# Coefficients of an eight-step graph layer from powers of one symmetric matrix, with an earlier load and a redrawn order of stages

## The reference

```python
# x: (16, 512, 128), adj: (512, 512); four layers, each followed by a layernorm
x = layernorm(x + L0(x))   # ((x + relu(G(relu(G(x)))))/2, G(x) = x W_loop + adj (x W_neigh) + b
x = layernorm(x + L1(x))
x = layernorm(x + L2(x))   # concat of x scaled by row sums (adj, adaptive softmax) @ W + b
x = layernorm(x + L3(x))   # attention over 256 edges: leaky_relu, segment softmax, scatter

# L1, with N_STEPS = 8
h = jnp.einsum('bnd,ed->bne', x, fc_in_w) + fc_in_b
w_eff = w * d_clamped @ w.T
dt = jnp.float32(SPATIAL_SCALE / N_STEPS)
def euler_step(h, _):
    ax = jnp.einsum('nm,bmd->bnd', adj_mx, h)
    f = alph * 0.5 * (ax - h) + h @ w_eff - h + x0
    return (h + dt * f, None)
h, _ = jax.lax.scan(euler_step, h, None, length=N_STEPS)
```

## Time and profile before

| | |
|---|---|
| median of 3 runs | 724.84 us (724.22 to 725.11) |
| profiled execution | 727.18 us, span 725.3 us |
| granted TensorE clock, mean | 0.901 |
| PE busy | 597.7 us (82%) |
| DVE busy | 466.0 us (64%) |
| ACT busy | 331.2 us (46%) |
| POOL busy | 220.2 us (30%) |

### The profile page before, as it was taken

How to read it: one execution, slowest core, us unless ns; L and a number is a source line. 1 busy time by engine, 2 the same in 40 slices (tenths; PEclk the granted TensorE clock), 3 DMA queues, 4 the chain that set the end, 5 groups by cost and what they waited for, 6 DMA issues and landing times.

```text
span 725.3 us, 9315 instructions
## 1 busy us (share of the span) xinstructions
PE 597.7 (82%) x3024; PEld 504.5 (70%) x3024; DVE 466.0 (64%) x1256; ACT 331.2 (46%) x777; POOL 220.2 (30%) x222
## 2 busy tenths in 40 slices
PE   2768849689999999996885859899999999785662
PEld 2556618558997889974774747789887998674541
DVE  6883677235464576537798779726639662678665
ACT  2661211464725367424285354663544752264132
POOL 1252502252216311232155343450552122302402
PEclk9897758789999999997898999999999999987676
DMA  7100000300000000211031110400000011001122
GB/s 221 33 0 30 0 1 0 117 1 0 2 1 1 1 1 1 83 34 59 3 114 59 58 59 1 117 1 1 1 0 1 1 67 51 0 1 59 58 58 59
DMA packets 28502, 24.61 MB, mean 34 GB/s; under 512 B 3739, under 2 KB 22683, under 8 KB 28453
## 3 DMA queue, kind: packets, MB, share of 16 engines
q1 hardware_dynamic: 27012, 19.25, 8.7%
...
...
## 4 chain that ended last, share of the span: by engine, by line
PE 60%; DVE 28%; ACT 5%; issue 3%; POOL 2%; DMA 1%; ACTq 0%; DVEq 0%; POOLq 0%
PE bank L1260 32%; PE bank L1542 11%; DVE stats L1076 6%; PE bank L1459 5%; PE bank L1458 4%; ACT ZH L624 2%; PE bank L1434 2%; PE bank L1446 1%; PE bank L1515 1%; POOL ZL L540 1%; DVE XF L1167 1%; DVE XF L1241 1%; PE bank L1328 1%; POOL small L563 1%; DVE XF L1094 1%
## 5 line engine op out<-in xcount | busy, mean ns | idle before, releaser
L563 POOL TENSOR_TENSOR small<-small,minus_half 128x8 f32<-128x8 f32 x32 | 55.1, 1722 | 314.4 <-DVE small L1069 314.4
L540 POOL TENSOR_TENSOR ZL<-XF,ZH 128x512 fp32r<-128x512 f32 x64 | 80.9, 1299 | 105.8 <-ACT ZH L624 105.8
L624 ACT ACTIVATE ZH<-bank 128x128 fp32r<-128x128 f32 (+1 forms) x112 | 35.8, 323 | 110.4 <-PE bank L1260 109.9
L1048 DVE TENSOR_TENSOR ZL<-bank,ZH 128x128 fp32r<-128x128 f32 (+1 forms) x112 | 37.7, 345 | 69.7 <-ACT XF L624 53.4
L813 ACT ACTIVATE XF<-XF,small 128x128 f32<-128x128 f32 x128 | 52.0, 486 | 53.1 <-POOL small L565 46.8
L1260 PE MATMUL bank<-QH,YR 128*128 128x384 f32 x256 | 75.9, 337 | 0.0
L1459 PE MATMUL bank<-ZL,BTH 128*128 128x512 f32 x192 | 74.3, 418 | 0.0
L1458 PE MATMUL bank<-ZH,BTH 128*128 128x512 f32 x144 | 61.0, 423 | 2.1 <-POOL ZL L540 2.0
L1076 DVE BATCH_NORM_STATS2 stats<-XF 128x6 f32<-128x128 f32 x256 | 55.8, 281 | 2.2
L1542 PE MATMUL bank<-ZH,RH 128*128 128x512 f32 x128 | 51.1, 399 | 1.7 <-POOL ZL L540 0.8
L1542 PE MATMUL bank<-ZH,RL 128*128 128x512 f32 x128 | 50.7, 396 | 0.0
...
## 6 DMA issues: line engine op xcount, KB each, us to landing
...
Z<-x_rows,ends_at POOLq DMA_INDIRECT x16, 3.5
...
```

The costliest lines, as they stand in the source:

```text
L540: g.tensor_tensor(lo, whole, raw(hi), ALU.subtract).then_inc(pool_done[s], 1)
L563: g.tensor_tensor(sm[:, 6, :], sm[:, 5, :], minus_half[:, :], ALU.pow).then_inc(pool_done[s], 1)
L624: return A.activation(out_, in_, ACT.Copy, **more)
L1048: ins = (v.tensor_tensor(lo, part, raw(hi), ALU.subtract) if shift is None else v.scalar_tensor_tensor(lo, part, shift, raw(hi), ALU.add, ...
```

## The change

- Powers. V2, V3 and V4, V5 to V8 are made as plain powers of V in three small stages, `w.pw0`, `w.pw1` and `w.pw2`, which stand apart from each other in the order. ACT copies each power, scaled by a binomial, into VC (eight copies). POOL fills SV with multiples of the identity at the very start. DVE adds the powers into SV with 28 instructions on 128 by 128 elements (`w_sums`, in its stage `w.q`).
- Q. PE makes each of the three lots of Q as one product of FCN with three blocks of VC and one of CENTRE with three of SV (384 columns each; the last lot is two blocks wide, and one block more with the identity). The banks are those of stream 0.
- `row_sum` moves on DVE from the end of `w.weights` to the end of `w.lmat`.
- Scratch of the preparation moves out of the buffer of x of group 1. SP issues that load at once behind the first loads, and its transposed twin at `w.one_hot`.
- The order is redrawn. In the preparation, `0.pair2` and `0.neigh2` stand ahead of `w.r3`, and `1.x0`, `1.t0` and `1.neigh1` stand ahead of `w.end`. In the middle of turn 0, `0.gather`, `0.qv` and `0.score` stand ahead of `1.giant2`. At the end of turn 1, `2.l2.b` alternates with `3.lot.b`, `2.norm.2` stands behind `3.lot.3`, and `2.gather` stands behind `3.giant2`.
- Some waits are added where buffers or banks are shared in a new way, among them `step1` of group 0 on DVE's "done" and `neigh1` of group 1 on `weights`.

```diff
--- before.py
+++ after.py
@@ -154,8 +157,8 @@
         regions = {"F1": flat(F[1]), "ZH1": flat(ZH[1]), "ZL1": flat(ZL[1]), "TH1": flat3(TH[1]),
-                   "TL1": flat3(TL[1]), "X1": flat(X[1]), "Y1": Y[1][:, :],
-                   "T1": T1[:, :], "Q": Q[:, :]}
+                   "TL1": XT[1][:, :], "X1": flat(X[1]), "Y1": Y[1][:, :],
+                   "Q": Q[:, :]}
...
-        in_order = """w.adj w.low w.w0 w.v 0.x0 w.lmat 0.t0 0.neigh1 w.r2 0.conv1 w.edges w.r3 w.rt w.powers w.one_hot
...
+        in_order = """w.adj w.low w.w0 0.x0 w.v w.lmat w.pw0 0.t0 0.neigh1 w.r2 w.pw1 0.conv1 w.edges 0.triple 0.stats.0
...
@@ -474,9 +474,10 @@
             load_weights("w")
             load_weights("ends")
-            def w_end():
-                sync.wait_ge(w_dve_done, after(w_dve_steps, 0, "done"))
-                load(1, 1)
+            load(1, 1)
+
+            def w_one_hot():
+                sync.wait_ge(w_dve_done, after(w_dve_steps, 0, "one_hot"))
                 load_t(1, 1)
@@ -533,6 +534,8 @@
+            for k in range(EULER_STEPS):
+                link(g.tensor_scalar(SV[:, k, :], ident[:, :], DT + (1.0 if k == 0 else 0.0), None, ALU.mult))
@@ -600,20 +603,9 @@
-            def w_q():
-                gp.wait_ge(w_dve_done, after(w_dve_steps, 0, "r_lo", NB - 1))
-                for factor in factors:
-                    link(g.tensor_scalar(ident_by[factor], ident[:, :], factor, None, ALU.mult))
@@ -684,9 +676,28 @@
+            def by_choice(p, src):
+
+                k = EULER_STEPS - p
+                copy(VC[:, k, :], src, scale=float(comb(EULER_STEPS, k))).then_inc(w_act_done, 1)
+
+            def w_pw0():
+                ac.wait_ge(w_dve_done, after(w_dve_steps, 0, "v"))
+                by_choice(1, V)
+                ac.wait_ge(w_dve_done, after(w_dve_steps, 0, "v2"))
+                by_choice(2, power[:, 0, :])
...
@@ -910,6 +926,7 @@
+                v.tensor_reduce(row_sum, adj_sb, AX, ALU.add).then_inc(w_dve_done, 1)
@@ -976,16 +993,36 @@
-            def w_powers():
...
+            def w_pw0():
+                dv.wait_ge(w_dve_done, after(w_dve_steps, 0, "row_sum"))
+                dv.wait_ge(w_pe_done, after(w_pe_steps, 0, "v2"))
+                v.tensor_copy(power[:, 0, :], w_bank[3][:, 0:D]).then_inc(w_dve_done, 1)
...
+            def w_sums():
+
+                nonlocal n
+                dv.wait_ge(w_pool_done, after(w_pool_steps, 0, "const"))
+                dv.wait_ge(w_dve_done, after(w_dve_steps, 0, "v8"))
+                for p in range(1, EULER_STEPS):
+                    if p > 1:
+                        dv.wait_ge(dve_chain, n)
+                    v_p = V if p == 1 else power[:, p - 2, :]
+                    for k in range(EULER_STEPS - p):
+                        v.scalar_tensor_tensor(SV[:, k, :], v_p, DT * comb(k + p, k), SV[:, k, :],
+                                               ALU.mult, ALU.add).then_inc(dve_chain, 1)
+                        n += 1
...
@@ -1004,7 +1041,7 @@
-                v.tensor_reduce(row_sum, adj_sb, AX, ALU.add).then_inc(w_dve_done, 1)
+                v.memset(tmp_c, 0.0).then_inc(w_dve_done, 1)
...
@@ -1353,68 +1395,65 @@
+            def w_pw0():
+                pt.wait_ge(w_dve_done, after(w_dve_steps, 0, "nv1_t"))
+                products(w_bank[3][:, 0:D], [(V, V)]).then_inc(w_pe_done, 1)
...
             def w_q():
-                pt.wait_ge(w_pool_done, after(w_pool_steps, 0, "q"))
-                pt.wait_ge(w_dve_done, after(w_dve_steps, 0, "t_sum", NB - 1))
...
                 for i in range(LOTS):
-                    for place in range(LOT):
-                        k = place * LOT + i
...
-                        last = products(w_bank[i][:, block_of(place)],
-                                        [(f_power, scaled(f_factor))]
-                                        + [(power(j - k, 1), scaled(factor)) for j, factor in parts])
+                    n = LOT if i < LOTS - 1 else LOT - 1
+                    last = products(q_bank(i)[:, 0:n * D], [(FCN, VC[:, i::LOT, :]), (CENTRE, SV[:, i::LOT, :])])
+                    if n < LOT:
+                        last = products(q_bank(i)[:, n * D:LOT * D], [(FCN, ident[:, :])])
...
+                if (turn, s, stage, i) == (0, 0, "step1", 0):
+                    pt.wait_ge(w_dve_done, after(w_dve_steps, 0, "done"))
+                if (turn, s, stage, i) == (0, 1, "neigh1", 0):
+                    pt.wait_ge(w_dve_done, after(w_dve_steps, 0, "weights"))
```

More of the change, by code:

```diff
@@ new lines, in w_numbered @@
+        def w_numbered(steps):
+            return numbered([one for name in in_order if name[:2] == "w." for one in steps.get(name[2:], [])])
+        w_dve_done = sem("w_dve_done")
+        w_dve_steps = w_numbered({
+            "adj": [("b_hi", NB), ("r_diag", 1)], "low": [("b_lo", NB), ("r_row", 1)], "w0": [("inexact", 1)],
+            "v": [("w_by_d", 1), ("v", 1), ("centred", 1), ("nv1_t", 1)],
+            "lmat": [("l_nat", NB), ("l_lo", NB), ("row_sum", 1)], "r2": [("l2", NB), ("l2_lo", NB)],
+            "edges": [("perm", 1), ("ends_row", 1), ("src_col", 1)], "r3": [("l3", NB)], "rt": [("r_lo", NB)],
+            "pw0": [("v2", 1)], "pw1": [("v4", 1)], "pw2": [("v8", 1)], "one_hot": [("one_hot", 1), ("l2_sum", 1)],
+            "q": [("sums", 1)], "weights": [("l2_w", 1), ("weights", 1)], "picked": [("picked", 1), ("log_in", 1)],
+            "soft": [("rowmax+t_sum", NB)], "end": [("done", 1)]})
@@ L502, in norm @@
                     store(s, turn)
-            run({"end": w_end, "x3": x3, "qv": qv, "norm": norm})
+            run({"one_hot": w_one_hot, "x3": x3, "qv": qv, "norm": norm})
             for s in range(STREAMS):
@@ L698, in x0 @@
                 ac.wait_ge(x_loaded[s], (turn + 1) * (16 * NB))
+                if (turn, s) == (0, 1):
+                    ac.wait_ge(w_pe_done, after(w_pe_steps, 0, "l3", NB - 1))
                 for a in range(NB):
@@ L712, in conv1 @@
             def conv1(turn, s):
+                if (turn, s) == (0, 1):
+                    ac.wait_ge(w_dve_done, max(after(w_dve_steps, 0, "picked"), after(w_dve_steps, 0, "t_sum", NB - 1)))
                 for b in range(GB):
@@ L1103, in neigh1 @@
             def neigh1(turn, s):
+                if (turn, s) == (0, 1):
+                    dv.wait_ge(w_pe_done, after(w_pe_steps, 0, "l2_mean", 1))
                 for b in range(GB):
@@ L1109, in pair2 @@
                 dv.wait_ge(y_stored[s], (turn + 1) * (16 * NB))
+                if (turn, s) == (0, 1):
+                    dv.wait_ge(w_pe_done, after(w_pe_steps, 0, "q_t", LOTS - 1))
                 for i in range(8):
@@ L1608, in scatter @@
                           needs=((act_done, act_steps, "wout_hi", GB - 1), (dve_done, dve_steps, "wout_lo", GB - 1)))
-            stages = {"adj": w_adj, "low": w_low, "w0": w_w0, "v": w_v, "edges": w_edges, "powers": w_powers,
+            stages = {"adj": w_adj, "low": w_low, "w0": w_w0, "v": w_v, "edges": w_edges, "pw0": w_pw0, "pw1": w_pw1, "pw2": w_pw2,
                       "r2": w_r2, "r3": w_r3, "rt": w_rt, "l2_mean": w_l2,
```

219 lines of the change are left out of this document (103 added, 116 removed).

## The result

The changed kernel takes 723.53 us (median of 13 runs, 722.31 to 726.00), the kernel before in the same session 725.85 (13 runs, 724.22 to 727.29): a ratio of 0.9971, 95% interval 0.9959 to 0.9983. It is faster, by 0.29%, half of the 0.58% of the forecast. The profiled execution took 724.18 us where that of before took 727.18.

The account below looks back on a forecast made before the run. PE was taken to bound the kernel from 172 to 300 us, the order of work elsewhere. +1.5 - 6.9 - 4.4 + 5.6 = -4.2 made 723.0 of the profiled 727.18, 720.6 of the median; range 713 to 727.

Parts of the forecast that it names:

- B: Start of `0.lot.0`: moving `1.neigh1` out of the PE-bound stretch gains 6.9 us (bounds 7.5 to 6).
- A: Preparation, up to PE's start of `0.step1`: 1.5 us later, at 137.1 (bounds -2 to +3.5).
- C: Middle of turn 0, to group 1's third layer: `0.gather`, `0.qv`, `0.score` ahead of `1.giant2` gain 4.4 us (bounds 0 to 7.6).
- the discount for the sums of `1.l2.0`: Middle of turn 0: these sums wait for ACT's copies, so 4.4 us of gain was taken, with the residual 5.7 earlier.
- the third rival: Middle of turn 0: `1.giant2` binds and its +6.05 us is carried whole, time 731.1 us; chance 0.13.
- I take 6.5 with the seven waits between powers: Preparation: DVE's 28 sums of powers take 6.5 us, between 6.1 and 8.1.
- the early delay: Start of the preparation: V squared comes 3.8 us later; +3.4 carried to the end of `w.edges` (bounds 2.3 and 3.8).
- the second rival: Preparation: DVE's sums wait for POOL's low parts and end 5.2 us later, A +6.7, time 725.8 us; chance 0.14.
- D: End of turn 1, to group 3's third layer: idle, a clock fall and `2.qv` cost 0.75 + 2.6 + 2.2, +5.6 us (0 to +6.2).
- The first rival: End of turn 1: the clock holds at `3.giant2`, D about +0.5, time 715.5 us; chance 0.25.
- Between these places: Stretches between the four landmarks: order nearly the same, so no shift was counted.

Follow-up runs that it names:

- e8: e4 with `1.x0`, `1.t0` and `1.neigh1` back behind `0.step2` as before the change, the load still early: 718.17 us.
- e7: e4 with the middle of turn 0, `1.giant1` to `0.scatter`, in the order of the kernel before: 724.92 us.
- e4: Changed kernel with `w.v` ahead of `0.x0`, and POOL's low parts of `1.x0` waiting until DVE's weights are done: 717.41 us.
- e3: Changed kernel with `w.v` ahead of `0.x0` again, nothing else altered: 720.25 us.
- e1: Changed kernel with POOL's low parts of `1.x0` waiting until DVE has finished the 28 sums: 723.4 us.
- e2: Changed kernel with POOL's low parts of `1.x0` waiting until DVE's weights are done: 721.2 us.
- e5: e4 with the end of turn 1, up to `2.score`, in the order of the kernel before: 717.64 us.
- e9: e4 with the steps of turn 0 from `0.lot.3` to `0.x3` in the order of the kernel before: 715.89 us.

## Why the prediction was right and wrong

**Right: B, by its mechanism and nearly its size.** PE between `0.step1` and `0.lot.0` is 7.9 us shorter, for 6.9: PE is busy 8.9 less, of which 7.55 are `1.neigh1`, and idle 1.0 more, where the forecast gave 0.65 back. That the same work costs the preparation 7.0 (e8) was in the forecast's running sum of A, but not held against B, so the forecast spoke of a gain of 6.9 where the move as a whole nets 0.8.

**Right in place and direction: C, larger than forecast, and in good part for a reason that it did not price.** 7.2 us on PE, and 7.5 by e7, where the forecast took 4.4 between bounds of 0 and 7.6. Counted from `0.gather`, `1.giant2` starts 8.8 later (323.78 less 315.00) where it was 2.3, so +6.45 for the forecast's +6.05, and its products cover DVE's scans: at 321.27 `0.score` has 1.03 of idle in place of 4.62. DVE's timeline of the changed kernel, the first residual of `0.scatter`:

```profile
349.38 0.68 DVE L1282 TENSOR_TENSOR XF<-bank,XF 128x512 f32<-128x512 f32 x1
```

It comes 34.4 behind the gather for 41.0 before, 6.6 earlier for the forecast's 5.7 (5.6 by its own 349.5). What failed was the discount for the sums of `1.l2.0`, which "wait for ACT's copies as well": they start at 357.32 for 363.06 before, as much earlier as the residual. The test that the prediction set (the residual 11 earlier in all) was missed, at 5.7, because A and B had brought the stage no forward shift, and not because `1.giant2` binds; the third rival was wrong. C is more than the whole gain of the changed kernel: with e7 undoing it, even the preparation of e4 leaves 725 us.

What the forecast did not price is the clock. Windows from `0.gather` to the third layer of group 1, before and after: length; PE, PEld, DVE, ACT, POOL busy; granted clock, DMA.

```profile
314.12:368.80 54.68, 43.82 (x215) 35.34 (x213) 38.49 (x116) 23.41 (x59) 13.43 (x12) 0.84 0.13 39
315.00:362.43 47.43, 39.45 (x215) 33.47 (x213) 39.13 (x116) 23.34 (x59) 14.15 (x12) 0.93 0.15 45
```

PE's idle shrinks by 2.9 us only (10.9 to 8.0; 4.43 is new ahead of `0.wout`). The other 4.4 are the same 215 products in less time, at a granted clock of 0.93 for 0.84: the eight of `0.score`, close behind other work, take 1.89 for 3.57. In e7 the stretch has 0.78 and 46.07 of PE, in e4 0.93 and 39.55. The forecast had worked with "the durations that these stages have now".

**Wrong: A, +7.0 for +1.5, outside its bounds of -2 to +3.5.** The step that failed is "I take 6.5 with the seven waits between powers", made of DVE durations from rows in which POOL was still: the 28 sums took 9.7. With it failed the 3.8 for the early delay, which is read from the order of before, `w.v` ahead of `0.x0`; with that order, in e3, `0.neigh1` starts at 29.26, near the forecast's 29.6. At the end of the sums the kernel was at 105.34 for 98.8, 6.5 late: 1.9 from `w.v` (`0.neigh1` at 31.51 for 29.6), where ACT's copies of x and POOL's low parts both stand in the way, 1.0 from the copy of L994, 3.2 from the seven sums (4.70 for 1.49), and 0.4 between. Behind the sums 1.0 came back. e1, e2 and e3 moved these, and e4 without them put `0.step1` at 137.10, with the steps on the way at the forecast's times (end of the sums 98.90 for 98.8, of the weights 104.16 for 103.9). The count of instructions and of their durations was right; their neighbour was missing.

That was the second rival. Its place and its mechanism came true, and its chance of 0.14 was too low. Its price of 5.2 for the sums was 4.2 with the copy; that A came to +7.0, near its +6.7, is owed to the 1.9 from `w.v` as well, which it did not count. The row it rested on, L896 of the earlier trace rows with 1.2 us for 128 by 128 elements, was such a meeting (26.99 to 28.19, beside POOL's low parts from 24.37 to 29.34). The Trainium skill ("SBUF — State Buffer", section "Who interferes with whom") says that VectorE and GpSimd share a pair of SBUF ports as an exclusive lock, that instructions with two SBUF inputs contend for it, and that copies, casts and `tensor_scalar` can. The rows agree on all of these kinds beside POOL's low parts (4.70 for seven sums, 1.29 for the copy, 1.44 for the cast, 0.92 for a `tensor_scalar`); beside L603 an addition with two SBUF inputs paid nothing (0.28), so for that pair the measurement differs. The prediction had written that by this rule the rival is the forecast, and then went by its chance instead. Its time of 725.8 was not reached because C and D came out better.

**Wrong in size: D, +2.2 for +5.6.** The idle ahead of `3.giant2` was foreseen (2.66, within 2.3 to 3.05, though the lower end does not follow from 613.6 and the 1.3 of one low part, which give 1.8), and the clock fell. What it cost was not. Windows of the changed kernel from 609 us: length; PE, PEld, DVE, ACT, POOL busy; granted clock, DMA.

```profile
609.00:613.00 4.00, 3.13 (x8) 2.54 (x9) 1.55 (x1) 0.43 (x1) 4.00 (x4) 0.57 0.04 14
613.00:618.00 5.00, 5.00 (x23) 4.01 (x22) 0.00 (x0) 0.00 (x0) 0.89 (x1) 1.00 0.00 0
```

Up to 613 the clock was mostly at its lower level, 1.2 GHz, and from 613 on at the upper one. At half clock the 3.1 us from 609.87 to 613 do 1.6 of work, so the fall cost at most some 1.6 us (an estimate from these rows), and not the 2.6 taken from `0.neigh2`. That stage was low for longer, though not throughout, as the forecast's "half clock" has it; a window of the kernel before, columns as above:

```profile
108.60:114.40 5.80, 5.80 (x15) 4.54 (x15) 3.83 (x13) 1.63 (x4) 0.00 (x0) 0.50 0.00 1
```

From 114.4 to its end at 118.8 the granted clock is 1.00. And the 2.2 for `2.qv` at half clock were mostly given back by `3.t2`: close behind `2.qv` its 16 products take 1.91 (at 633.97), where before they stood behind 6.26 us of idle and took 3.67. e5 with the old order has that 3.67 again, and its `3.l2.0` comes at 634.75, 0.95 before e4's; in the times nothing is left of it. The first rival, that the clock holds, was wrong, although D came out between it and the forecast.

**Wrong: "Between these places the order is nearly the same, and I count nothing there".** The stretch from 172 to 300 had its own reordering, and `0.lot.0` to `0.gather` grew by 1.7 us, in part in the small idles at 261.43 and 290.60. The ten traces with the changed order have 143.8 to 144.2 here, the two with the order of before 142.2 and 142.5 (e9). Those two idles, 0.36 and 0.58, are gone in e9 and account for 0.9 of the 1.6 against e4; the rest lies in PE's busy time and stays unexplained.
